# A graph network on one core: the last two gather passes, the first by step instead of by chunk, with a ring of 24 rows, one-hots 12 steps ahead and no spare product

## The chip, the core and the metric

One core of one Trainium2 chip runs the whole program. The metric is the time of one execution on the device in microseconds (us), as the median of several runs. The engines are TensorE (PE; its weight loads are PEld), VectorE (DVE), ScalarE (ACT), GpSimd (POOL) and SyncE (SP). SP and POOL also issue DMAs, POOL the indexed ones.

## The reference

A graph of 6250 nodes and 106,250 edges (50,000 drawn pairs in both directions and one loop for each node, sorted by the target `dst`) goes through four layers, each followed by a residual sum and a layer norm: a graph isomorphism layer, an attention over edges, a layer of degree and edge terms, and the layer that the change is about, which is, shortened:

```python
def _srgnn_conv(x, W, b, src, dst, num_nodes):
    xl = x @ W.T + b
    agg = segment_sum(xl[src], dst, num_segments=num_nodes)
    cnt = segment_sum(ones, dst, num_segments=num_nodes)
    return agg / maximum(cnt, 1.0)[:, None]
input_in  = _srgnn_conv(hidden, W_in,  b_in,  src, dst, n)
input_out = _srgnn_conv(hidden, W_out, b_out, dst, src, n)
# then the gates of a recurrent unit from inputs = [input_in, input_out] and hidden
```

All data is fp32 and 256 wide.

## The kernel before

Eleven stages run one after the other, each ended by a barrier. Four of them gather a row of 256 (or 512) numbers for every edge with indexed DMAs of POOL: `first_gather`, `edge_scores`, and `last_gathers` twice. `last_gathers` makes both sums of the layer above: the inward pass (rows of `src` summed by `dst`) and the outward pass (rows of `dst` summed by `src`).

**Chunks, blocks and steps.** The sorted edges lie in NC = 832 chunks of 128. The nodes lie in NW = 49 blocks of 128. A step adds one chunk's share of one block; a chunk that reaches into the next block takes a second step. There are STEPS = 880 steps in a pass (55 groups of U = 16).

**One step of a pass.** POOL gathers 128 rows (128 KB) into one place of `ring` (line 2083). DVE compares a row of 0 to 127 with the edges' node numbers and so makes four one-hot matrices at once (`hot`, which calls `compare`, line 195). PE multiplies the one-hot with the gathered rows and adds to the block's bank in PSUM (line 2126, tile `l_sums`). An fp32 product is two records of the trace. After each product PE makes a spare product of one column (`push`, line 178) whose result nobody reads. ACT copies a finished block's sum out of PSUM and clears the bank (`take_banks`, lines 186 and 188).

**The inward pass goes by chunk.** POOL gathers 832 chunks, each once, though some serve two steps. Which place of the ring a step reads, and when it may, follow from the block's number in a register (`slot_of`, `chunk_ready`, line 154). SP is the relay: for each chunk it waits for the row, tells PE through `s_here` (line 137), and, eight chunks later, waits for the last step that used the chunk and tells POOL through `s_used` (line 148).

**The outward pass goes by step.** POOL gathers 880 times, PE waits for the row's own semaphore, and POOL waits for `s_sum`, PE's count of steps. In this pass PE, DVE and SP also make the gates for one block in each group of 16 steps (`gate_parts`: four transposes L2027, four products of 512 columns L2039, four of 256 columns L2042; DVE L1999, L2005, L1982, L1994, L2011; a 512 KB write by SP).

**What limits how far the engines run ahead.** The ring has 16 places and POOL asks at every fourth gather, so it is at most 16 and at least 13 gathers ahead of what is used up. `onehot` has HALF = 8 places and DVE makes four of them 4 steps before PE's use:

```python
if u % QUAD == 0 and t + QUAD < 2 * STEPS:
    hot(t + QUAD)
```

Of the kernel before, what the change touches and what calls it, by code (L numbers as in the profile page):

```python
# [12 lines left out]
P = 128  # L13
# [148 lines left out]
def bank_of(block, width):  # L162

    return bass.ds((block % BANKS) * BANK, width)
# [7 lines left out]
    pe.sem_inc(s_sum, 1)  # L172


def push(pe, k, spare):

    ones = k.ones.bitcast(BF16)
    pe.matmul(spare, ones[:, 0:1], ones[:, 0:1], start=True, stop=True)  # L178


def take_banks(act, k, ends, sums, width, place, s_sum, s_taken, s_free, turn=0):

    for w in range(NW):
# [14 lines left out]
def step_tables(nc, k, dst_rows, src_rows, x_rows):  # L198
# [4 lines left out]
    with ExitStack() as ctx:  # L203
# [34 lines left out]
        @block.sync  # L238
        def _(sp):

            sp.dma_start(last_i[:, :], dst_rows[:, P - 1:P].rearrange("c o -> o c"),
                         allow_slow_non_contiguous=True).then_inc(s_last, 16)
            sp.dma_start(k.X, x_rows.rearrange("(w p) d -> p w d", p=P)).then_inc(s_x, 16)

            sp.dma_start(k.src_p, k.src_rows).then_inc(s_x, 16)
            sp.dma_start(k.by_chunk, k.src_cols).then_inc(s_x, 16)
            sp.wait_ge(s_lasts, 4)
            sp.dma_start(k.last_row, k.lasts).then_inc(s_x, 16)
            sp.wait_ge(s_rel, 3 * RT)
# [4 lines left out]
            sp.wait_ge(s_x, 64)  # L254

        @block.gpsimd
        def _(pool):
# [1276 lines left out]
def attr_sums(nc, k):  # L1534

    RING = 4
    with ExitStack() as ctx:
# [6 lines left out]
        s_zeros, s_one, s_src, s_rel, s_hot, s_sum, s_taken, s_free, s_sources = sems(  # L1544
            nc, k, *(f"as_{n}" for n in ("zeros", "one", "src", "rel", "hot", "sum", "taken", "free", "sources")))
# [4 lines left out]
        @block.sync  # L1550
        def _(sp):
            for q in range(BIN_OCTS):
                if q >= RING:
                    sp.wait_ge(s_sum, (q - RING + 1) * OCT + 1)
                    sp.wait_ge(s_src, 2 * (q - RING + 1))
                sp.dma_start(ring[:, q % RING, :, 0:ER], k.bin_rows[q * OCT * P:(q + 1) * OCT * P, :].rearrange(
                    "(p r) d -> p r d", p=P)).then_inc(s_in[q % RING], 16)
            sp.dma_start(k.idx[:, 0:NC], k.src_cols).then_inc(s_sources, 16)
            sp.wait_ge(s_sources, 16)

        @block.scalar
        def _(act):
# [485 lines left out]
    return work  # L2048


def last_gathers(nc, k, a):

    with ExitStack() as ctx:
        room = Arena(k.side)
        ring = room.take([P, U, D])
        flat = ring.rearrange("p u d -> p (u d)")
        onehot = room.take([P, HALF, P])
        lasts_row = room.take([1, NC], I32)
        zeros = room.take([1, BANK])
        sums = psum(nc, ctx, "l3_sums", [P, BANKS * BANK])  # L2060
        spare = psum(nc, ctx, "l3_spare", [1, BANK])
        s_zeros, s_hot, s_sum, s_taken, s_free, s_lasts, s_here, s_used = sems(nc, k, *(f"l3_{n}" for n in (
            "zeros", "hot", "sum", "taken", "free", "lasts", "here", "used")))
        s_row, row0 = k.s_row, k.rows_before
        k.rows_before += NC + 16 * IT
# [5 lines left out]

        @block.gpsimd
        def _(pool):
            for n in range(NC + STEPS):
                u = n % U
                column = k.idx[:, n:n + 1] if n < NC else k.idx2[:, n - NC:n - NC + 1]
                if u % QUAD == 0 and n >= U:

                    if n < NC + U:
                        pool.wait_ge(s_used, n + QUAD - U)  # L2080
                    else:
                        pool.wait_ge(s_sum, STEPS + (n - NC) + QUAD - U + 1)
                pool.indirect_dma_start(ring[:, u, :], None, k.x3_rows, bass.IndirectOffsetOnAxis(  # L2083
                    ap=column, axis=0)).then_inc(s_row[u], 16)

        @block.sync
        def _(sp):
            sp.dma_start(lasts_row, k.last_row).then_inc(s_lasts, 16)
            fold.sync(sp)
            work.load_bias(sp)  # L2090
            sp.sem_inc(s_here, HERE)
            sp.wait_ge(s_lasts, 16)
            lasts = None
            for c in range(NC):
                lasts = relay_chunk(nc, sp, lasts, lasts_row, c, s_row, row0, s_here, s_sum, s_used)
            for c in range(NC - BEHIND, NC):
                lasts = relay_used(nc, sp, lasts, lasts_row, c, s_sum, s_used)
            work.sync(sp)

        @block.scalar  # L2100
# [7 lines left out]
        def _(pe):  # L2108
# [4 lines left out]
            for t in range(2 * STEPS):  # L2113
# [12 lines left out]
                pe.matmul(sums[:, bank_of(node[u] + turn, D)], onehot[:, u % HALF, :], flat[:, bass.ds(at, D)],  # L2126
                          start=False, stop=True, skip_group_check=True).then_inc(s_sum, 1)
# [6 lines left out]
        def _(dve):  # L2134
            def hot(t):

                node = (k.dst if t < STEPS else k.rel2)[:, t % STEPS:t % STEPS + QUAD]
                if t >= HALF:
                    dve.wait_ge(s_sum, t + QUAD - HALF + 1)
                compare(dve, k, onehot[:, t % HALF:t % HALF + QUAD, :], None, node).then_inc(s_hot, QUAD)  # L2140
# [190 lines left out]
def build(nc, k, a):  # L2331
    with ExitStack() as ctx:
# [11 lines left out]
        k.last_row = dram("last_row", [1, NC], I32).ap()  # L2344
# [115 lines left out]
```

## Time and profile before

| what | value |
|---|---|
| median of 3 runs | 6660.27 us (6643.98 to 6661.23) |
| profiled execution, its own time, first to last instruction | 7527.2 us |
| first gather | 60 to 1360 us |
| edge scores | 1942 to 3275 us |
| edge attribute sums (no gathers of POOL) | 4283 to 4591 us |
| inward pass | 4803 to 6037 us |
| outward pass | 6037 to 7327 us |

The profiled execution is one execution with the profiler on; nothing lies around its span but the launch. It took 867 us more than the median of the runs without the profiler. In every list a group of instructions has its busy time, the mean duration of one in ns, and the idle time of its engine just before it, with what ended that idle time. "issue" means that the profile shows nothing that was waited for. The granted clock of TensorE is 1.0 at 2.4 GHz and 0.5 at 1.2 GHz.

### The profile page before, as it was taken

The numbers are of one execution on the slowest core, as the hardware profiler recorded it, in microseconds if no ns is written. First come the engines' busy times: TensorE is split into PE (matmuls) and PEld (weight loads), VectorE is DVE, ScalarE is ACT, GpSimd is POOL, SyncE is SP. The second block draws the span as 40 slices with busy tenths as digits, with TensorE's granted clock in tenths as the row PEclk, the third lists the DMA queues.
The fourth block names the chain that finished last, engine by engine and source line by source line (L and its number), as shares of the span: only waits on it lengthen the run. The fifth ranks groups of instructions, "written<-read, shape, count | busy, mean of one in ns | idle before, by whom it ended". The sixth has DMA issues, their size and how long they took to land. (4 is left out here: it accounts for less than half of the span.)

```text
span 7527.2 us, 81611 instructions
## 1 busy us (share of the span) xinstructions
PE 5373.7 (71%) x17807; PEld 3065.0 (41%) x17807; DVE 3160.7 (42%) x6956; ACT 545.2 (7%) x1542; POOL 4732.4 (63%) x4778
## 2 busy tenths in 40 slices
PE   5666777638765556636566687788888888888887
PEld 2333333525332223324444575433433344444444
DVE  2222444528655556674444567511111123333317
ACT  0000000324000000010000001100000000000004
POOL 5666665664666666677677404766666666666665
PEclk8777777969767777767778899865555588888869
DMA  4444433331688888846667675433333333333445
GB/s 137 133 134 130 124 123 121 128 100 66 214 256 256 265 262 268 266 134 210 210 217 226 205 191 148 126 89 89 90 89 87 89 111 119 119 119 119 123 101 191
DMA packets 693161, 1164.20 MB, mean 155 GB/s; under 512 B 104128, under 2 KB 490285, under 8 KB 692614
## 3 DMA queue, kind: packets, MB, share of 16 engines
q0 software_dynamic: 224288, 633.55, 28.9%
q1 hardware_dynamic: 468344, 525.21, 21.9%
q8 instruction: 217, 3.56, 0.2%
q14 instruction: 202, 1.65, 0.1%
q10 hardware_dynamic: 110, 0.23, 0.0%
HBM read 870.83 MB, written 287.77 MB: 154 GB/s over the span
## 5 line engine op out<-in xcount | busy, mean ns | idle before, releaser
L2126 PE MATMUL l_sums<-big 128*128 (+1 forms) x3520 | 1701.9, 578 | 349.1 <-issue 135.1
L195 DVE TENSOR_TENSOR big<-iota_row,dst_tab 128x512 f32<-128x512 f32 x660 | 458.4, 695 | 2171.3 <-PE l_sums L2126 712.1
L1280 POOL DMA_INDIRECT bin_rows<-staging,place_tab x832 | 979.6, 1177 | 337.4 <-issue 249.1
L1166 POOL DMA_INDIRECT big<-kv_rows,idx_tab x880 | 832.0, 945 | 503.0 <-issue 241.1
L578 POOL DMA_INDIRECT big<-in_x,big x832 | 826.6, 994 | 483.6 <-SPq L148 237.7
L2083 POOL DMA_INDIRECT big<-x_rows,place_tab x880 | 882.3, 1003 | 394.9 <-issue 241.7
L2083 POOL DMA_INDIRECT big<-x_rows,idx_tab x832 | 817.2, 982 | 426.7 <-issue 226.6
L1220 PE MATMUL es_q<-big 128*128 x1760 | 720.9, 536 | 450.3 <-issue 343.3
L2126 PEld LDWEIGHTS l_sums<-big 128*128 128x128 f32 x3520 | 765.2, 259 | 502.0 <-issue 473.7
L612 PE MATMUL l_sums<-big 128*128 x1760 | 723.0, 543 | 331.9 <-issue 235.8
L1504 PE MATMUL ws_sums<-big 128*128 128x264 f32 x1760 | 546.1, 474 | 321.2 <-DVE big L1524 170.9
L1220 PEld LDWEIGHTS es_q<-big 128*128 128x128 f32 x1760 | 380.6, 252 | 747.7 <-issue 714.1
L612 PEld LDWEIGHTS l_sums<-big 128*128 128x128 f32 x1760 | 393.8, 255 | 623.9 <-issue 587.7
L1239 DVE TENSOR_TENSOR big<-es_q,big 128x256 f32<-128x256 f32 x880 | 370.8, 423 | 547.4 <-remote 274.3
L1504 PEld LDWEIGHTS ws_sums<-big 128*128 128x128 f32 x1760 | 400.6, 236 | 467.7 <-issue 384.9
L178 PEld LDWEIGHTS l_spare<-ones 128*1 128x1 bf16 x1760 | 139.7, 79 | 906.7 <-issue 906.7
L1244 DVE TENSOR_REDUCE sims<-big 128x8 f32<-128x256 f32 x880 | 356.1, 410 | 0.0
L1524 DVE TENSOR_TENSOR big<-big,sims 128x1024 f32<-128x1024 f32 x220 | 268.7, 1221 | 180.5 <-DMA big<-v_edge 173.6
L195 DVE TENSOR_TENSOR big<-iota_row,bin_tab 128x512 f32<-128x512 f32 x220 | 151.8, 692 | 440.4 <-PE l_sums L2126 263.8
L178 PE MATMUL l_spare<-ones 128*1 128x1 bf16 x1760 | 289.3, 164 | 3.4 <-issue 3.4
L1581 PE MATMUL as_sums<-sims 128*128 128x129 f32 x1760 | 249.8, 298 | 56.2 <-DVE sims L195 54.9
L1581 PEld LDWEIGHTS as_sums<-sims 128*128 128x128 f32 x1760 | 232.8, 189 | 74.5 <-issue 67.9
(297 smaller groups left out, 5187.4 us busy)
## 6 DMA issues: line engine op xcount, KB each, us to landing
v_edge<-big SPq DMA_DIRECT2D x880, 128.0 KB
big<-v_edge SPq DMA_DIRECT2D x220, 512.0 KB
bin_rows<-big SPq DMA_DIRECT2D x110, 520.0 KB
sims<-bin_rows SPq DMA_DIRECT2D x110, 520.0 KB
staging<-in_edges SPq DMA_DIRECT2D x104, 520.0 KB
gate_rows<-big SPq DMA_DIRECT2D x49, 512.0 KB
big<-gate_rows SPq DMA_DIRECT2D x49, 512.0 KB
big<-kv_rows,idx_tab POOLq DMA_INDIRECT x880
```

The lines of the kernel that those rows point to most:

```text
L178: pe.matmul(spare, ones[:, 0:1], ones[:, 0:1], start=True, stop=True)
L195: return dve.tensor_tensor(out, rows, columns.unsqueeze(2).to_broadcast([P, QUAD, P]), ALU.is_equal)
L578: pool.indirect_dma_start(ring[:, u, 0:D], None, table, bass.IndirectOffsetOnAxis(ap=k.by_chunk[:, c:c + 1], axis=0)).then_inc(s_row[u], 16)
L612: pe.matmul(sums[:, bank_of(node[u], width)], onehot[:, u % HALF, :], flat[:, bass.ds(slot_of(s, node[u], D + 1), width)], start=False, st ...
L1166: pool.indirect_dma_start(ring[:, u, :], None, k.kv_rows, bass.IndirectOffsetOnAxis(ap=k.idx[:, s:s + 1], axis=0)).then_inc(s_row[u], 16)
L1220: pe.matmul(qps[u % 4][:, 0:D], onehot[:, u % HALF, :], query[:, bass.ds(block_at[u] * D, D)], start=True, stop=True).then_inc(s_q, 1)
L1239: dve.tensor_tensor(prod[:, u % 2, :], qps[u % 4][:, 0:D], ring[:, u, 0:D], ALU.mult).then_inc(s_prod, 1)
L1280: pool.indirect_dma_start(k.bin_rows, bass.IndirectOffsetOnAxis(ap=k.place[:, c:c + 1], axis=0), k.staging[:, g % 2, j, :], None).then_inc ...
L1504: pe.matmul(sums[:, bank_of(node[s % U], AW)], onehot[:, s % HALF, :], weighted[:, s % HALF, :], start=False, stop=True, skip_group_check= ...
L1581: pe.matmul(sums[:, bank_of(node[s % U], EW)], onehot[:, s % U, :], ring[:, q % RING, r, 2:2 + EW], start=False, stop=True, skip_group_che ...
L2083: pool.indirect_dma_start(ring[:, u, :], None, k.x3_rows, bass.IndirectOffsetOnAxis(ap=column, axis=0)).then_inc(s_row[u], 16)
L2126: pe.matmul(sums[:, bank_of(node[u] + turn, D)], onehot[:, u % HALF, :], flat[:, bass.ds(at, D)], start=False, stop=True, skip_group_check ...
```

## The change

- The inward pass goes by step, as the outward pass does: POOL gathers 880 rows, not 832, from the table of steps (`idx_tab`, which held the steps' rows for an earlier stage and is no longer overwritten with the chunks'). SP relays nothing, so `relay_chunk`, `relay_used`, the row `last_row` and its loads are gone from this stage. The first gather keeps its relay.
- The ring has 24 places instead of 16 in both passes, each with a semaphore of its own, and POOL asks `s_sum` at every fourth gather.
- There are 16 one-hots instead of 8, and DVE makes them 12 steps ahead instead of 4.
- The spare product is gone from both passes.

```diff
@@ last_gathers @@
-        ring = room.take([P, U, D])
+        ring = room.take([P, LAST_RING, D])          # 24
-        onehot = room.take([P, HALF, P])
-        lasts_row = room.take([1, NC], I32)
+        onehot = room.take([P, LAST_HOTS, P])        # 16
...
         @block.gpsimd
         def _(pool):
-            for n in range(NC + STEPS):
-                u = n % U
-                column = k.idx[:, n:n + 1] if n < NC else k.idx2[:, n - NC:n - NC + 1]
-                if u % QUAD == 0 and n >= U:
-                    if n < NC + U:
-                        pool.wait_ge(s_used, n + QUAD - U)
-                    else:
-                        pool.wait_ge(s_sum, STEPS + (n - NC) + QUAD - U + 1)
-                pool.indirect_dma_start(ring[:, u, :], None, k.x3_rows, ...).then_inc(s_row[u], 16)
+            for t in range(2 * STEPS):
+                place = t % LAST_RING
+                column = k.idx[:, t:t + 1] if t < STEPS else k.idx2[:, t - STEPS:t - STEPS + 1]
+                if place % QUAD == 0 and t >= LAST_RING:
+                    pool.wait_ge(s_sum, t + QUAD - LAST_RING + 1)
+                pool.indirect_dma_start(ring[:, place, :], None, k.x3_rows, ...).then_inc(s_row[place], 16)
...
         def _(sp):
-            sp.dma_start(lasts_row, k.last_row).then_inc(s_lasts, 16)
             fold.sync(sp)
             work.load_bias(sp)
-            sp.sem_inc(s_here, HERE)
-            sp.wait_ge(s_lasts, 16)
-            lasts = None
-            for c in range(NC):
-                lasts = relay_chunk(nc, sp, lasts, lasts_row, c, s_row, row0, s_here, s_sum, s_used)
-            for c in range(NC - BEHIND, NC):
-                lasts = relay_used(nc, sp, lasts, lasts_row, c, s_sum, s_used)
             work.sync(sp)
...
-                if turn:
-                    pe.wait_ge(s_row[u], row0 + NC + 16 * ((t - STEPS) // U + 1))
-                else:
-                    chunk_ready(pe, t, node[u], s_here)
-                at = u * D if turn else slot_of(t, node[u], D)
+                pe.wait_ge(s_row[t % LAST_RING], 16 * (t // LAST_RING + 1))
+                at = t % LAST_RING * D
...
-                push(pe, k, spare[:, 0:1])
...
             def hot(t):
-                if t >= HALF:
-                    dve.wait_ge(s_sum, t + QUAD - HALF + 1)
+                if t >= LAST_HOTS:
+                    dve.wait_ge(s_sum, t + QUAD - LAST_HOTS + 1)
...
-            hot(0)
+            for t in range(0, LAST_LEAD, QUAD):      # LAST_LEAD = 12
+                hot(t)
...
-                if u % QUAD == 0 and t + QUAD < 2 * STEPS:
-                    hot(t + QUAD)
+                if u % QUAD == 0 and t + LAST_LEAD < 2 * STEPS:
+                    hot(t + LAST_LEAD)
@@ attr_sums, the stage that overwrote idx_tab @@
-            sp.dma_start(k.idx[:, 0:NC], k.src_cols).then_inc(s_sources, 16)
-            sp.wait_ge(s_sources, 16)
@@ step_tables @@
-            sp.wait_ge(s_lasts, 4)
-            sp.dma_start(k.last_row, k.lasts).then_inc(s_x, 16)
```

On POOL the two passes stood in this order before (`idx_tab` is the inward pass, `place_tab` the outward one):

```order
L2083 DMA big<-x_rows,idx_tab 128x256 x832
L2083 DMA big<-x_rows,place_tab 128x256 x880
```

and now:

```order
L2072 DMA big<-x_rows,idx_tab 128x256 x880
L2072 DMA big<-x_rows,place_tab 128x256 x880
```

Nothing else moved on POOL; the inward pass has 48 gathers more.

On PE, in the middle of the inward pass before, two steps (the register instructions find the place in the ring, the bank and the waits' values):

```order
L154 REGISTER_ALU x3
L2125 REGISTER_ALU
L2126 ISA x2
L2126 MATMUL l_sums<-big 128x256
L178 MATMUL l_spare<-ones 1x1
L154 REGISTER_ALU x3
L2125 REGISTER_ALU
L2126 ISA x2
L2126 MATMUL l_sums<-big 128x256
L178 MATMUL l_spare<-ones 1x1
```

and now the same two steps:

```order
L2103 REGISTER_ALU
L2104 ISA
L2104 MATMUL l_sums<-big 128x256
L2103 REGISTER_ALU
L2104 ISA
L2104 MATMUL l_sums<-big 128x256
```

The spare product and four register instructions of each step are gone; the order of the products is as it was.

On DVE, the start of the stage before, where L1976 waits for the biases that SP loads:

```order
L2142 MEMSET big 1x512
L195 TENSOR_TENSOR big<-iota_row,dst_tab 128x512
L1976 TENSOR_TENSOR big<-big 128x512
L195 TENSOR_TENSOR big<-iota_row,dst_tab 128x512 x8
L1916 TENSOR_SCALAR xs<-ones,xs 128x128 x4
```

and now:

```order
L2120 MEMSET big 1x512
L189 TENSOR_TENSOR big<-iota_row,dst_tab 128x512 x3
L1966 TENSOR_TENSOR big<-big 128x512
L189 TENSOR_TENSOR big<-iota_row,dst_tab 128x512 x8
L1906 TENSOR_SCALAR xs<-ones,xs 128x128 x4
```

Two more groups of one-hots stand ahead of the first wait, and so every later group stands 8 steps further ahead of its use.

## Rows read from the trace of the kernel before

**Rows 1.** The head of the page.

```profile
span 7527.2 us, 81611 instructions
```

**Rows 2.** Busy PE, PEld, DVE, ACT, POOL by stretch; granted clock, DMA share, GB/s.

```profile
4283.00:4591.00 308.00, 250.65 (x1762) 232.81 (x1760) 188.05 (x542) 26.26 (x98) 0.00 (x0) 0.99 0.72 188
4803.00:6037.00 1234.00, 1047.77 (x2667) 490.21 (x2667) 161.14 (x242) 35.88 (x96) 817.06 (x832) 0.56 0.32 92
6037.00:7190.00 1153.00, 972.88 (x3371) 523.29 (x3370) 359.25 (x587) 33.64 (x90) 797.05 (x794) 0.86 0.40 118
7190.00:7327.00 137.00, 111.72 (x282) 51.88 (x280) 17.23 (x26) 3.57 (x10) 85.38 (x87) 0.55 0.50 88
```

**Rows 3.** The page, costliest groups: POOL's four gather passes.

```profile
L1166 POOL DMA_INDIRECT big<-kv_rows,idx_tab x880 | 832.0, 945 | 503.0 <-issue 241.1
L578 POOL DMA_INDIRECT big<-in_x,big x832 | 826.6, 994 | 483.6 <-SPq L148 237.7
L2083 POOL DMA_INDIRECT big<-x_rows,place_tab x880 | 882.3, 1003 | 394.9 <-issue 241.7
L2083 POOL DMA_INDIRECT big<-x_rows,idx_tab x832 | 817.2, 982 | 426.7 <-issue 226.6
```

**Rows 4.** Who waited for whom, over both passes (us, times, longest).

```profile
DVE big L195 <- PE l_sums L2126: 975.9, 248, 12.4
POOL big L2083 <- SPq L148: 192.5, 95, 6.3
```

**Rows 5.** Timeline of the inward pass, at the granted clock 0.5.

```profile
5316.14 1.22 PE L2126 MATMUL l_sums<-big 128*128 x2
5317.29 0.08 PEld L178 LDWEIGHTS l_spare<-ones 128*1 128x1 bf16 x1 [0.65 <-issue]
5317.39 1.22 PE L2126 MATMUL l_sums<-big 128*128 x2
```

**Rows 6.** Timeline of PE in the first gather, four steps each (x8).

```profile
1000.68 3.72 PE L612 MATMUL l_sums<-big 128*128 x8
1005.34 2.09 PE L612 MATMUL l_sums<-big 128*128 x8
```

**Rows 7.** Timeline of the outward pass: start, duration, [idle before <- what ended it].

```profile
6397.04 0.59 PE L2126 MATMUL l_sums<-big 128*128 128x256 f32 x2
6398.81 0.70 PE L2042 MATMUL gp_g<-sims,big 128*128 128x256 f32 x2
6398.99 0.94 POOL L2083 DMA_INDIRECT big<-x_rows,place_tab  x1 [0.30 <-issue]
6399.97 0.70 PE L2042 MATMUL gp_g<-sims,big 128*128 128x256 f32 x2
6401.12 0.70 PE L2126 MATMUL l_sums<-big 128*128 128x256 f32 x2
6402.49 0.69 DVE L195 TENSOR_TENSOR big<-iota_row,bin_tab 128x512 f32<-128x512 f32 x1 [0.77 <-PE l_sums L2126]
6402.66 1.34 POOL L2083 DMA_INDIRECT big<-x_rows,place_tab  x1 [2.73 <-PE l_sums L2126]
6403.67 0.86 PE L2126 MATMUL l_sums<-big 128*128 128x256 f32 x2 [1.75 <-DVE big L195]
...
6412.02 1.13 PE L2039 MATMUL gp_g<-sims,big 128*128 128x512 f32 x2
6413.60 1.12 PE L2039 MATMUL gp_g<-sims,big 128*128 128x512 f32 x2
6423.69 0.70 PE L2126 MATMUL l_sums<-big 128*128 128x256 f32 x2
6424.41 0.70 PE L2126 MATMUL l_sums<-big 128*128 128x256 f32 x2
```

**Rows 8.** Timeline of the end of the outward pass.

```profile
7313.40 0.94 POOL L2083 DMA_INDIRECT big<-x_rows,place_tab  x1 [0.30 <-issue]
7325.14 1.22 PE L2126 MATMUL l_sums<-big 128*128 128x256 f32 x2 [0.37 <-DMA big<-x_rows,place_tab]
```

More of the change, by code:

```diff
@@ L172, in clear_banks @@
     pe.sem_inc(s_sum, 1)
-def push(pe, k, spare):
-    ones = k.ones.bitcast(BF16)
-    pe.matmul(spare, ones[:, 0:1], ones[:, 0:1], start=True, stop=True)
 def take_banks(act, k, ends, sums, width, place, s_sum, s_taken, s_free, turn=0):
@@ L253, in _ @@
             sp.wait_ge(s_rows, 48)
-            sp.wait_ge(s_x, 64)
+            sp.wait_ge(s_x, 48)
         @block.gpsimd
@@ L1543, in attr_sums @@
         sums = psum(nc, ctx, "as_sums", [P, BANKS * BANK])
-        s_zeros, s_one, s_src, s_rel, s_hot, s_sum, s_taken, s_free, s_sources = sems(
-            nc, k, *(f"as_{n}" for n in ("zeros", "one", "src", "rel", "hot", "sum", "taken", "free", "sources")))
+        s_zeros, s_one, s_src, s_rel, s_hot, s_sum, s_taken, s_free = sems(
+            nc, k, *(f"as_{n}" for n in ("zeros", "one", "src", "rel", "hot", "sum", "taken", "free")))
         s_in = sems(nc, k, *(f"as_in{n}" for n in range(RING)))
@@ L2048, in gate_parts @@
     return work
+LAST_RING = 24
+LAST_HOTS = 16
+LAST_LEAD = 12
 def last_gathers(nc, k, a):
@@ L2054, in last_gathers @@
         room = Arena(k.side)
-        ring = room.take([P, U, D])
+        ring = room.take([P, LAST_RING, D])
         flat = ring.rearrange("p u d -> p (u d)")
-        onehot = room.take([P, HALF, P])
-        lasts_row = room.take([1, NC], I32)
+        onehot = room.take([P, LAST_HOTS, P])
         zeros = room.take([1, BANK])
         sums = psum(nc, ctx, "l3_sums", [P, BANKS * BANK])
[L2061 to L2065, printed above, removed]
+        s_zeros, s_hot, s_sum, s_taken, s_free = sems(nc, k, *(f"l3_{n}" for n in (
+            "zeros", "hot", "sum", "taken", "free")))
+        s_row = sems(nc, k, *(f"l3_row{n}" for n in range(LAST_RING)))
         k.gate = gate_weights(k)
@@ L2073, in _ @@
         def _(pool):
-            for n in range(NC + STEPS):
-                u = n % U
-                column = k.idx[:, n:n + 1] if n < NC else k.idx2[:, n - NC:n - NC + 1]
-                if u % QUAD == 0 and n >= U:
-                    if n < NC + U:
-                        pool.wait_ge(s_used, n + QUAD - U)
-                    else:
-                        pool.wait_ge(s_sum, STEPS + (n - NC) + QUAD - U + 1)
-                pool.indirect_dma_start(ring[:, u, :], None, k.x3_rows, bass.IndirectOffsetOnAxis(
-                    ap=column, axis=0)).then_inc(s_row[u], 16)
+            for t in range(2 * STEPS):
[3 more added lines that the diff above has]
+                    pool.wait_ge(s_sum, t + QUAD - LAST_RING + 1)
+                pool.indirect_dma_start(ring[:, place, :], None, k.x3_rows, bass.IndirectOffsetOnAxis(
+                    ap=column, axis=0)).then_inc(s_row[place], 16)
         @block.sync
         def _(sp):
-            sp.dma_start(lasts_row, k.last_row).then_inc(s_lasts, 16)
             fold.sync(sp)
             work.load_bias(sp)
-            sp.sem_inc(s_here, HERE)
-            sp.wait_ge(s_lasts, 16)
-            lasts = None
-            for c in range(NC):
-                lasts = relay_chunk(nc, sp, lasts, lasts_row, c, s_row, row0, s_here, s_sum, s_used)
-            for c in range(NC - BEHIND, NC):
-                lasts = relay_used(nc, sp, lasts, lasts_row, c, s_sum, s_used)
             work.sync(sp)
@@ L2125, in _ @@
                 pe.wait_ge(s_free, (node[u] & NODE_BITS) + turn * NW)
-                pe.matmul(sums[:, bank_of(node[u] + turn, D)], onehot[:, u % HALF, :], flat[:, bass.ds(at, D)],
+                pe.matmul(sums[:, bank_of(node[u] + turn, D)], onehot[:, t % LAST_HOTS, :], flat[:, bass.ds(at, D)],
                           start=False, stop=True, skip_group_check=True).then_inc(s_sum, 1)
-                push(pe, k, spare[:, 0:1])
                 fold_beside(t)
@@ L2137, in hot @@
                 node = (k.dst if t < STEPS else k.rel2)[:, t % STEPS:t % STEPS + QUAD]
-                if t >= HALF:
-                    dve.wait_ge(s_sum, t + QUAD - HALF + 1)
-                compare(dve, k, onehot[:, t % HALF:t % HALF + QUAD, :], None, node).then_inc(s_hot, QUAD)
+                if t >= LAST_HOTS:
+                    dve.wait_ge(s_sum, t + QUAD - LAST_HOTS + 1)
+                at = t % LAST_HOTS
+                compare(dve, k, onehot[:, at:at + QUAD, :], None, node).then_inc(s_hot, QUAD)
             dve.memset(zeros[:, :], 0.0).then_inc(s_zeros, 1)
-            hot(0)
+            for t in range(0, LAST_LEAD, QUAD):
+                hot(t)
             fold_beside = fold.vector(dve)
@@ L2343, in build @@
         k.bin_rows = dram("bin_rows", [STEPS * P, ER]).ap()
-        k.last_row = dram("last_row", [1, NC], I32).ap()
         k.edge_rows, k.src_rows, k.src_cols = a["edges"], a["src_p"], a["src_c"]
```

## The prediction

> **What bounds the kernel now.** I read the stretches first. In the inward pass POOL is busy 817 of 1234 us and PE 1048, at a mean granted clock of 0.56; in the outward pass it is 797 and 973 of 1153, at 0.86 [rows 2]. Neither is full, so the question is what each waits for.
>
> *POOL's own pace.* A gather that nothing disturbs takes 0.945 us and the next starts 0.30 us later [rows 3, 7], so POOL can't go faster than one gather in 1.246 us. The inward pass adds 817.2 - 832 x 0.946 = 30 us of longer gathers and 426.7 - 832 x 0.30 = 177 us of idle time; the outward pass adds 50 and 131 [rows 3].
>
> *PE's own pace.* At the clock 0.5 a step repeats every 1.25 us (5316.14, 5317.39): the product, then 0.65 us in which the spare's weight load waits, then the spare [rows 5]. At full clock it repeats every 0.72 us [rows 7]. The first gather makes the same product with 257 columns and no spare product: four steps in 3.72 us, 0.93 each, and in 2.09, 0.52 each [rows 6]. So the spare product costs PE 0.32 us a step at the lower clock and 0.20 at the higher, though it computes for only a moment: it stands between a product and the next weight load, which otherwise runs early.
>
> *Whose signals come late.* The gather at 6402.66 stood idle for 2.73 us, and what it waited for is the product that began at 6397.04, so was over at 6397.63: the signal took five us. The compare at 6402.49 and PE's own next product (1.75 us idle at 6403.67) hang on late signals too [rows 7]. Compares waited 976 us for products in these passes, up to 12.4 us at a time [rows 4]. In the stage without gathers PE makes its 880 steps in 308 us at a clock of 0.99 [rows 2], with nothing of the kind. POOL's idle time above 0.30 us a gather is, over its four gather passes, 239 + 234 + 131 + 177 = 781 us [rows 3]. And the profiled execution is 867 us longer than the median of the runs [rows 1]. I read these together: most of the late signals belong to the execution with the profiler on, and the timed runs don't have them. I can't see what delays a signal; POOL's gathers are what the stages with late ones share. It is an inference from two near sums, and the first rival below is that it is wrong. So I make the sum twice.
>
> **The change, on the recorded execution.** If the deeper ring and the longer lead let POOL run without any idle time above 0.30 us, the passes take 880 x 1.246 = 1096 us each, plus longer gathers of 32 and 50: 1128 and 1146. Then some 4 us follow until the last product is done, an estimate from the wait of one gather and one product; now it is 13 (its product starts 11.7 us after the last gather's start and takes 1.2), and it waited for its row, so that signal was late too [rows 8]. Before, the two passes took 1234 and 1290 [rows 2]. In all 1234 + 1290 - 1128 - 1146 - 4 = 246 us less, 7527 - 246 = 7281. But a longer ring doesn't remove late signals, it rides over them. If POOL still needs the outward pass's present 1.45 us a gather ((882 + 395) / 880, [rows 3]), the inward pass takes 880 x 1.45 = 1276, and it is near 7560. I expect the record between, near 7450, and don't rest the prediction on it.
>
> **The change, in the timed runs.** I take the recorded durations and leave the late signals out.
>
> *Inward pass, before.* POOL needs 832 x 1.246 + 30 = 1067 us. PE needs 880 x 1.25 = 1100 at the lower clock, which it has for most of the pass (mean 0.56). So it takes between 1067 and 1100; I take 1085, as some stretches at full clock let PE catch up. *After.* PE needs 880 x 0.93 = 818 at most, POOL 1096 + 32 = 1128. The 48 gathers more cost 60 us on the engine that now sets the pace. Change **+43** (from +28 to +61). The relay's removal saves SP's work and four register instructions a step on PE, none of it on the path once POOL is it: 0.
>
> *Outward pass, before.* A group of 16 steps costs PE at full clock 4 x 1.58 (6412.02 to 13.60, a step with 512 columns of gates) + 4 x 1.16 (6398.81 to 99.97) + 8 x 0.72 [rows 7] and about 1 for the transposes, 17.7 us; at half clock about 1.7 times that, 30. At the mean clock 0.86 (0.72 of the time full) this is 1 / (0.72/17.7 + 0.28/30) = 20.0 us; the busy time says 973/49 = 19.9 [rows 2]. POOL needs 16 x 1.246 + 0.9 = 20.8. These are near each other, and one-hots only 4 steps ahead add small waits: I take 1165 for the pass (1147 if POOL alone decides, 1277 if all waits are real). *After.* Without the spare product PE's group is 17.7 - 3.2 = 14.5 at full clock, near 16.6 in the same mix, well under POOL's 20.8. The pass is POOL's 1147. Change **-18** (from 0 to -130).
>
> *Tail.* The last product's wait was for a late signal [rows 8]; without it PE is as near behind POOL before as after. **0** (to -8).
>
> *Longer gathers.* The gather at 6402.66 took 1.34 us where others take 0.94; a compare had started 0.17 us before it and ended at 6403.18 [rows 7]. The trace shows that a gather that starts inside a compare is held. The 30 and 50 us above are this. The next phase of compares against gathers I can't read off: with none held it is -32 and -50, with each of the 220 compares of a pass holding one by 0.5 us it is +80 and +60. I take **0**: the present rate. The Trainium skill (SBUF — State Buffer, "Who interferes with whom") says a VectorE instruction with two SBUF inputs contends with a GpSimd instruction that reads SBUF and that the loser is blocked; the rows agree, and this would not change the sum.
>
> *The rest.* The load of `idx_tab` that is dropped from the attribute sums was SP's last work there, beside PE's products (that stage has PE busy for 251 of 308 us): 0; uncovered it would be 2 us. The two earlier groups of one-hots cost DVE 1.4 us behind the clearing of the banks: 0. Eight more semaphores to clear at the barrier: 0.
>
> Sum: +43 - 18 + 0 + 0 = **+25**, so 6660 + 25 = **6685 us**, with its own range from 6640 to 6750.
>
> **Rivals.**
> - *The late signals are in every run* (not slower). For it: they are real time in the record, and nothing in the trace says what causes them. Against it: the runs are 867 us shorter, which must come from somewhere, and 781 us lies there. Then the recorded sum holds, -246 at best: about 6420. It makes the change faster once more than 45 of the 308 us of excess idle time in these two passes (177 + 131) are in the timed runs too. Chance 0.13.
> - *PE was further behind than I think in the outward pass.* If PE's group took 21.8 us, the pass was 1200 and the change gains 50 there; with the inward +28 the sum is -30: 6630. For it: PE busy 84% in the record. Chance 0.08.
> - *A gather costs less when it isn't recorded*, say 1.15 us. Then PE set both passes before (1100 and 19.9 x 49 + 120 = 1095) and POOL sets them after (1044 and 1062): about -90, 6570. Against it: the other two gather passes would be shorter by another 160 us, and 781 already fills most of the 867. Chance 0.05.
> - *Every compare holds a gather*: +140, 6800. Chance 0.04.
> - *The clock falls without the spare product.* Then PE takes 14.5 x 1.75 = 25 us a group in the outward pass against 20.8, 49 x 4.6 = +225: 6910. For it: the clock is 0.5 where PE has only the plain steps. Against it: there the spare product was made too, and the clock was still 0.56, and in the last stretch 0.55 with PE busy 112 of 137 us [rows 2]; the spare adds one column to some thousand. It decides if the outward pass's mean clock falls under 0.65. The rule of the Trainium skill that speaks for it (TensorE: Matmul & The Clock Gate, "Why this matters for your kernels": keep TensorE continuously busy, leave no long idle gaps) would have the engine's new idle time bring the clock down. Chance 0.04.
> - The forecast: 0.66.
>
> **The numbers.** Within 0.3% (20 us) is what a measurement of this kernel can't tell from no change. The forecast's own spread puts 0.40 of its 0.66 above +20, 0.24 within, 0.02 below. With the rivals: slower 0.40 + 0.08 = 0.48; same 0.24 + 0.02 = 0.26; faster 0.13 + 0.06 + 0.05 + 0.02 = 0.26. The range from 6510 to 6770 leaves out the late signals in every run (0.13), the clock (0.04) and most of the case of held gathers.
>
> **What would show it.** In the profile after: undisturbed gathers of 0.945 us with 0.30 between them in both passes (steps right), 1760 of them; PE steps every 0.93 us or less when they stand close, no L178; POOL's wait for `s_sum` rarer than before. Wrong would be: mean clock of the outward pass under 0.65; mean gather above 1.03 us; or a time near 6420, which says that the waits that I took for the profiler's are the kernel's.

## The result, and the profile after

The changed kernel takes **6700.5 us** (median of 5 runs, 6682.7 to 6707.4) against 6660.3: a ratio of **1.0064** with a 95% interval of 1.0047 to 1.0082, so 31 to 55 us more. The forecast was 6685. Its profiled execution took 6704.6 us, as long as its timed runs, which the one of before (7527.2) did not. So a second record was taken of the unchanged kernel; it took 6654.7 us, and from here "before" means that record, unless rows of the first are named. A record is called quiet when its span is near 6650 or 6700 us and not near 7500.

Changed kernel: the page's head, then two lines of who waited for whom (us, times, longest), which answer to [rows 1, 4]:

```profile
span 6704.6 us, 72065 instructions
DVE big L189 <- PE l_sums L2104: 1392.3, 374, 6.9
POOL big L2072 <- PE l_sums L2104: 34.7, 114, 0.3
```

POOL's 114 waits for PE are none of them longer than 0.3 us, the idle time that stands before every gather anyway. In [rows 4] it waited for SP's relay up to 6.3 us at a time.

Changed kernel: POOL's four gather passes by group (busy, mean ns | idle, what ended it), against [rows 3]:

```profile
L1158 POOL DMA_INDIRECT big<-kv_rows,idx_tab x880 | 832.1, 946 | 283.1 <-issue 224.0 <-SPq L1168 28.0 <-DVE big L1231 15.8
L570 POOL DMA_INDIRECT big<-in_x,big x832 | 831.1, 999 | 269.7 <-issue 244.0 <-POOLq L108 16.5 <-SPq L148 9.1
L2072 POOL DMA_INDIRECT big<-x_rows,place_tab x880 | 857.4, 974 | 268.1 <-issue 245.9 <-PE l_sums L2104 22.2
L2072 POOL DMA_INDIRECT big<-x_rows,idx_tab x880 | 837.1, 951 | 285.6 <-issue 255.3 <-POOLq L108 17.8 <-PE l_sums L2104 12.5
```

All four passes, also the two whose code is unchanged, now have 0.30 to 0.33 us idle a gather, counting the one wait of 10 to 18 us at the start of a stage; in [rows 3] the unchanged ones had 503.0 and 483.6 us. The unchanged kernel's second record says the same:

```profile
L2083 POOL DMA_INDIRECT big<-x_rows,place_tab x880 | 871.2, 990 | 268.2 <-issue 243.5 <-PE l_sums L2126 24.7
L2083 POOL DMA_INDIRECT big<-x_rows,idx_tab x832 | 797.8, 959 | 262.8 <-issue 249.6 <-POOLq L108 9.6 <-SPq L148 3.7
```

So POOL set the pace of both passes before and after, and a pass is as long as its gathers. The relay's 3.7 us are 12 waits of 0.3 us, so it held nothing up. The view of one line's instructions gives min/median/max ns and the first and the last start. Before, inward and outward:

```profile
L2083 POOL DMA_INDIRECT big<-x_rows,idx_tab x832: 942/947/1463, 4245.5 to 5295.5; - x167
L2083 POOL DMA_INDIRECT big<-x_rows,place_tab x880: 942/947/1461, 5296.8 to 6434.9; - x176
```

and in the changed kernel:

```profile
L2072 POOL DMA_INDIRECT big<-x_rows,idx_tab x880: 942/946/2582, 4261.1 to 5365.0; - x176
L2072 POOL DMA_INDIRECT big<-x_rows,place_tab x880: 942/946/1460, 5366.3 to 6490.5; - x176
```

From the first start to the next pass's first: inward 1051.3, now 1105.2, **+53.9**. First to last start outward: 1138.1, now 1124.2, **-13.9**. From the last gather's start to ACT's copy of the last sum: 17.1, now 14.3, **-2.8**:

```profile
6452.02 0.37 ACT L186 COPY xs<-l_sums 128x256 f32<-128x256 f32 x1 [62.64 <-PE l_sums L2126]
```
```profile
6504.84 0.37 ACT L180 COPY xs<-l_sums 128x256 f32<-128x256 f32 x1 [60.88 <-PE l_sums L2104]
```

The sum is +37, inside the measured 31 to 55. Of the 49.9 us between the two records 15.6 lie ahead of these passes (4261.1 against 4245.5). No cost of the change shows in that: the quiet records of all kernels reach this point between 4240.4 and 4261.1 us, and the changed kernel's own second record (experiment 10) at 4249.8.

A sum of two terms gives all four passes. One is the number of gathers times 1.249 us, the spacing of gathers that nothing holds (0.945 and 0.304). The other is what the longer gathers have above 0.946 us, added up in the trace: 11.3 and 39.3 us before, 5.4 and 25.5 in the changed kernel. That makes 1050, 1138, 1105 and 1125 us, against 1051, 1138, 1105 and 1124 measured. One gather in the changed kernel took 2.58 us. It stands first in the inward pass, beside the three compares in a row that the longer lead puts there (experiment 4 has it too), and makes 1.6 of the 5.4 us.

Last, the same two stretches before and after (busy PE, PEld, DVE, ACT, POOL; granted clock; DMA share; GB/s), against [rows 2]:

```profile
4245.00:5296.00 1051.00, 972.44 (x2687) 460.30 (x2687) 162.63 (x244) 35.88 (x96) 797.31 (x832) 0.64 0.38 108
5296.00:6452.00 1156.00, 1037.44 (x3629) 551.24 (x3629) 379.97 (x611) 36.62 (x98) 871.67 (x881) 0.87 0.45 128
```
```profile
4261.00:5366.00 1105.00, 938.09 (x1811) 416.69 (x1812) 163.05 (x246) 35.87 (x96) 837.10 (x880) 0.62 0.37 108
5366.00:6505.00 1139.00, 920.89 (x2746) 562.40 (x2745) 378.40 (x609) 36.77 (x99) 857.40 (x880) 0.81 0.45 130
```

PE has 117 us less to do outward, and the clock is 0.81 instead of 0.87. Neither shows in the time beyond POOL's 14 us. At the lower clock PE's closest steps are now 0.85 us apart, where before the most frequent distance was 1.24. So the spare product did cost PE time, but time that PE had.

### The profile page after: what moved, and what is told of

It reads as the page before. It is cut to its first block and busy times, and to the rows that moved or that the text cites. A ratio compares the mean times of both kernels' runs of the same rounds, so it can differ in the third digit from the quotient of the medians.

```text
span 6704.6 us, 72065 instructions
## 1 busy us (share of the span) xinstructions
PE 5133.2 (77%) x16047; PEld 2981.3 (44%) x16047; DVE 3169.9 (47%) x6956; ACT 545.6 (8%) x1542; POOL 4753.1 (71%) x4826
## 5 line engine op out<-in xcount | busy, mean ns | idle before, releaser
L2104 PE MATMUL l_sums<-big 128*128 128x256 f32 x3520 | 1594.1, 563 | 384.7 <-DMA big<-x_rows,place_tab 157.0
L1272 POOL DMA_INDIRECT bin_rows<-staging,place_tab x832 | 995.9, 1197 | 284.3 <-issue 249.2
L2072 POOL DMA_INDIRECT big<-x_rows,place_tab x880 | 857.4, 974 | 268.1 <-issue 245.9
L2072 POOL DMA_INDIRECT big<-x_rows,idx_tab x880 | 837.1, 951 | 285.6 <-issue 255.3
L1212 PE MATMUL es_q<-big 128*128 x1760 | 760.9, 564 | 191.4 <-DVE big L1231 188.0
L1496 PEld LDWEIGHTS ws_sums<-big 128*128 128x128 f32 x1760 | 410.3, 241 | 426.7 <-issue 338.7
L1673 POOL DMA_INDIRECT big<-in_L_gnn_z_in,sims x49 | 47.2, 962 | 346.8 <-DVE sims L1765 331.1
L180 ACT COPY big<-l_sums 128x257 f32<-128x257 f32 (+1 forms) x98 | 36.6, 373 | 2124.6 <-PE l_sums L2104 1076.3
```

Of the source, the lines that this page charges most:

```text
L1212: pe.matmul(qps[u % 4][:, 0:D], onehot[:, u % HALF, :], query[:, bass.ds(block_at[u] * D, D)], start=True, stop=True).then_inc(s_q, 1)
L1272: pool.indirect_dma_start(k.bin_rows, bass.IndirectOffsetOnAxis(ap=k.place[:, c:c + 1], axis=0), k.staging[:, g % 2, j, :], None).then_inc ...
L1496: pe.matmul(sums[:, bank_of(node[s % U], AW)], onehot[:, s % HALF, :], weighted[:, s % HALF, :], start=False, stop=True, skip_group_check= ...
L2072: pool.indirect_dma_start(ring[:, place, :], None, k.x3_rows, bass.IndirectOffsetOnAxis(ap=column, axis=0)).then_inc(s_row[place], 16)
L2104: pe.matmul(sums[:, bank_of(node[u] + turn, D)], onehot[:, t % LAST_HOTS, :], flat[:, bass.ds(at, D)], start=False, stop=True, skip_group_ ...
```

## The experiments

Every kernel ran beside the kernel before on one chip, 5 to 12 runs each. Ratios are to that kernel, with 95% intervals. In two of the four groups the kernel before took 6659.2 and 6653.4 us, in the other two 7518.2 and 7520.7 in all of its runs (7486 to 7572). They are kept apart, and "quiet chip" below means one of the first two groups, "late chip" one of the other two.

**1. The kernel before, unchanged (before_again).**

> The kernel before, unchanged, for a record that may be free of late signals, as the one of the changed kernel is. My theory (the late signals belong to one execution with the profiler on): time 6660 within 0.3%, and if this record is quiet too its span is near 6660, with POOL idle 0.30 to 0.34 us a gather in all four gather passes. Inward pass 1067 to 1100 us (PE at half clock with the spare product sets it: PE's step 1.25 us, POOL waits for PE or for SP's relay often), outward pass 1147 to 1180. First rival (POOL set the inward pass before as well): 832 x 1.255 = 1044 to 1050 us inward, and the outward pass longer by as much, 1170 to 1190. Second rival (late signals are in every execution of the kernel before): the record is near 7500 again.

Ratio 0.9996 (0.9987 to 1.0005). The record is the quiet one read above. Inward 1051 and not 1067 to 1100: the first rival holds there, though the outward pass was 1138 and not longer. The theory's 1067 to 1100 falls.

**2. Going by step alone (by_step_only).** The changed kernel with `LAST_RING = 16`, `LAST_HOTS = 8`, `LAST_LEAD = 4` and the spare product:

```diff
+                push(pe, k, spare[:, 0:1])
```

> The first part alone: inward pass by step, 880 gathers, no relay; ring of 16, one-hots 4 steps ahead and spare product as before. My theory: 48 more gathers, of which 17 us hidden before by PE's slower step (PE 1100, POOL 1067); but PE still needs 1.25 us a step at half clock and POOL 1.255, so they are level: +28 to +50 us, 6690 to 6710. First rival (POOL set the inward pass before): +60 us, 6720. Second rival (the relay was a cost of its own, so that without it the pass wins more than 48 gathers cost): at or below 6660.

6715.6 us, **1.0084** (1.0070 to 1.0098), +56 (47 to 65). The passes:

```profile
L2079 POOL DMA_INDIRECT big<-x_rows,idx_tab x880: 942/946/1462, 4260.0 to 5364.3; - x176
L2079 POOL DMA_INDIRECT big<-x_rows,place_tab x880: 942/946/1461, 5365.5 to 6503.8; - x176
```

1105.5 and 1138.3: +54 and 0. The first rival holds: 48 gathers cost their full 60 us (48 x 1.249), less the 6 us by which held gathers cost less (0.952 a gather against 0.959). PE is busy 1050 of the 1105 us at a clock of 0.57, so it is nearly the bound, but POOL never waited for it more than 0.3 us.

**3. The spare product alone (before_no_spare).**

```diff
-                push(pe, k, spare[:, 0:1])
```

> The last part alone on the kernel before: no spare product in the two passes. My theory: PE's step falls from 1.25 to 0.93 us at half clock, so the inward pass becomes POOL's 832 x 1.246 + 30 = 1067 (18 less) and the outward pass loses 10 to 18: 6625 to 6645. First rival (POOL set both passes anyway): 0, 6660. Second rival (the clock falls without the spare): outward pass longer, 6700 to 6850, with a mean granted clock under 0.65 there.

6648.7 us, 0.9987 (0.9978 to 0.9996), -9 (-15 to -3).

```profile
L2082 POOL DMA_INDIRECT big<-x_rows,place_tab x880 | 858.2, 975 | 268.2 <-issue 243.5 <-PE l_sums L2125 24.4 <-SPq L148 0.3
L2082 POOL DMA_INDIRECT big<-x_rows,idx_tab x832 | 804.8, 967 | 263.8 <-issue 251.4 <-POOLq L108 10.6 <-SPq L148 1.8
```

The idle time is as before. What moved is the length of a gather: 0.990 to 0.975 us outward (-13.0) and 0.959 to 0.967 inward (+7.0). So in these passes the spare product's work on PE cost no time; its removal moves when the compares begin against the gathers. The trace counts it: outward, the gathers lengthened by a compare have 11.0 us above 0.946 us instead of 24.9, inward 17.3 instead of 10.3, and those lengthened by the gates' instruction hardly change (14.2 against 13.6). Neither the theory nor a rival said that. The clock rival falls: 0.83 outward, and inward the mean clock is higher without the spare product (0.71 against 0.64), with PE busy 814 us instead of 972.

**4. The spare product and the longer lead (before_lead_no_spare).** As 3, with 16 one-hots and

```diff
-                if u % QUAD == 0 and t + QUAD < 2 * STEPS:
-                    hot(t + QUAD)
+                if u % QUAD == 0 and t + 12 < 2 * STEPS:
+                    hot(t + 12)
```

> The last two parts on the kernel before, by chunk and with the relay and the ring of 16: one-hots 12 steps ahead in 16 places and no spare product. If my sum is right in its parts (+43 for going by step, -18 for the rest of the outward pass, and 18 of PE's slack inward), this keeps the gains and not the price: 6620 to 6640, faster than both kernels. First rival (POOL alone set both passes, the ring and the lead give nothing): 6655 to 6665. Second rival (the longer lead itself costs, as more compares run while a gather's descriptors are written): 6670 to 6700.

6651.2 us, 0.9988 (0.9979 to 0.9997). The passes are those of 3:

```profile
L2082 POOL DMA_INDIRECT big<-x_rows,idx_tab x832: 942/946/2582, 4261.1 to 5318.3; - x167
L2082 POOL DMA_INDIRECT big<-x_rows,place_tab x880: 942/946/1474, 5319.6 to 6444.8; - x176
```

The lead gives 0. The outward pass is 1125.2 us, with the ring of 24 in the changed kernel 1124.2: the ring gives 0 (or 1 us) as well, as far as two kernels that differ in the inward pass too can tell. The last stretch takes 15.1 to 17.2 us in the quiet records with the ring of 16 (experiment 9 apart), and 14.3 and 14.5 in the two of the changed kernel, so 1 to 3 us are left for the ring.

**5 to 7. One part of the change undone at a time (after_spare, after_ring16, after_lead4).**

```diff
-LAST_RING = 24      # after_ring16
+LAST_RING = 16
-LAST_HOTS = 16      # after_lead4, both lines
+LAST_HOTS = 8
-LAST_LEAD = 12
+LAST_LEAD = 4
```

> The changed kernel with the spare product back in both passes; ring 24 and one-hots 12 ahead stay. Changed kernel 6700. My theory (POOL sets both passes and PE has room): PE's step is 1.25 us at half clock against POOL's 1.255, so the inward pass stays or grows by up to 10 us, and the outward pass grows by 0 to 20: 6700 to 6725. Rival (the clock gate: the spare keeps the clock up): mean granted clock higher than 0.62 inward and 0.81 outward and the time under 6690.

> The changed kernel with the ring cut back to 16 places. My theory: POOL waits for PE rarely with either (35 us in all in the changed kernel's record), a row needs about 3 us of 16 x 1.255 = 20 us of ring, so inward 0, and outward up to +20 where PE's groups of gates (17 us in a burst) let it fall behind: 6700 to 6720. Rival (the ring does nothing): 6700 within 0.15%. Rival (a longer ring costs, as more rows are in flight and gathers land later): under 6690.

> The changed kernel with one-hots 4 steps ahead in 8 places again. My theory: PE waits for compares a little in the outward pass, where DVE also serves the gates, and makes it up since it has room: 0 to +15, 6700 to 6715. Rival (the lead moves the compares against the gathers: with 12 steps ahead they start at another phase and hold more or fewer gathers): the mean gather moves off 0.951 inward and 0.974 outward by 0.01 us or more, 9 us of time a pass for each 0.01.

These three met a late chip (the kernel before takes 7518.2 us). Ratios: 1.0027 (1.0011 to 1.0043), 1.0000 (0.9981 to 1.0018), 1.0024 (1.0006 to 1.0041). So they say nothing of parts of 10 us at 6700, but overturned my reading of the first record: its 7527 us were no effect of the profiler. That is the kernel's time there. Whether it is the chip or something about it at that time, the runs don't tell.

One thing beside POOL's idle time sets these records apart: how long a register instruction of PE's own sequencer takes. Over the changed kernel's two passes, first on a late chip (the third record, experiment 12), then on a quiet one (min/median/max ns):

```profile
L2104 PEldq FUSED_REGOPS  x1760: 2/88/1401, 4797.2 to 7309.2; - x196
L2104 PEldq FUSED_REGOPS  x1760: 79/84/110, 4269.4 to 6503.4; - x196
```

In the whole program 105 to 277 of these instructions take over 0.3 us in each of the six late records, and none over 0.13 us in the eight quiet ones. Around 5002 to 5008 us of the first, each takes 0.70 us and PE's steps start 2.80 us apart. So PE itself runs late there, and not only the news of its products. Whether that is the cause or one more effect is open.

**8. Compares with one SBUF input (before_psum_rows).** As 3, and the row of 0 to 127 lies in the freed PSUM bank:

```diff
+            dve.tensor_copy(count_ps[:, 0:P], k.iota_row[:, :]).then_inc(s_count, 1)
+            dve.wait_ge(s_count, 1)
...
-                compare(dve, k, onehot[:, t % HALF:t % HALF + QUAD, :], None, node).then_inc(s_hot, QUAD)
+                compare(dve, k, onehot[:, t % HALF:t % HALF + QUAD, :],
+                        count_ps[:, 0:P].unsqueeze(1).to_broadcast([P, QUAD, P]), node).then_inc(s_hot, QUAD)
```

> The kernel before without the spare product, and the row of 0 to 127 that the compares of the two passes read copied once into the PSUM bank that this frees, so that a compare has one SBUF input instead of two. Theory (a gather that begins inside a compare with two SBUF inputs is held, and that is all that separates the passes of the kernels apart from their number of gathers): the longer gathers vanish (19 us inward, 27 outward in the record without the spare product alone), passes of 832 x 1.2488 = 1039 and 880 x 1.2488 = 1099 us, 6648 - 46 = 6602. Where a chip shows late signals the gathers still fall to 0.945 us, the time by less. Rival (any compare at work holds a gather, whatever its inputs): no difference from the kernel without the spare product, 6648. The Trainium skill (SBUF, section Who interferes with whom) says that a VectorE instruction with at most one SBUF input doesn't contend with GpSimd, which is the theory.

6616.0 us, **0.9934** (0.9920 to 0.9947), 33 us less than the 6648.7 of kernel 3, which was timed in another group beside nearly the same time of before. First what a held gather is: one of experiment 3 beside a compare, and one of the changed kernel beside the gates' instruction (DVE's row, then POOL's):

```profile
5296.98 0.69 DVE L195 TENSOR_TENSOR big<-iota_row,dst_tab 128x512 f32<-128x512 f32 x1 [3.76 <-PE l_sums L2125]
5297.28 1.21 POOL L2082 DMA_INDIRECT big<-x_rows,idx_tab  x1 [0.31 <-issue]
...
5815.39 0.75 DVE L1972 SCALAR_TENSOR_TENSOR big<-sims,big 128x512 f32<-128x512 f32 x1
5815.61 1.36 POOL L2072 DMA_INDIRECT big<-x_rows,place_tab  x1 [0.30 <-issue]
```

Each of the two gathers began inside a DVE instruction with two SBUF inputs and ended 0.82 us after that instruction's end (5297.67 and 5298.49; 5816.14 and 5816.97). Now a compare of this experiment, whose row comes from `l_count` in PSUM, with a gather that begins as far inside it as in the first pair, 0.30 us:

```profile
5019.65 0.69 DVE L195 TENSOR_TENSOR big<-l_count,dst_tab 128x512 f32<-128x512 f32 x1 [3.24 <-PE l_sums L2126]
5019.95 0.95 POOL L2083 DMA_INDIRECT big<-x_rows,idx_tab  x1 [0.30 <-issue]
```

That gather takes 0.95 us. The distance matters: a gather that begins together with a compare isn't held even with two SBUF inputs. In experiment 3 one began 0.02 us after its compare, at 4590.91, and took 0.95 us. Over the passes:

```profile
L2083 POOL DMA_INDIRECT big<-x_rows,idx_tab x832: 942/946/958, 4251.1 to 5289.9; - x167
L2083 POOL DMA_INDIRECT big<-x_rows,place_tab x880: 942/946/1472, 5291.1 to 6403.1; - x176
```

Inward the longest of 832 gathers took 0.958 us, and the pass 1040.0 us (forecast 1039). To count the same thing in both kernels, take the gathers of both passes that began at least 0.10 us after a compare's start and at least 0.20 us before its end. In experiment 3 there are 124, and all of them took over 1.0 us; here there are 117, and none did. Outward the pass is 1112.0 us and not 1099: the gates' `SCALAR_TENSOR_TENSOR` (L1982) still has two SBUF inputs, and 50 of the 57 long gathers began inside it. The other 7 began inside a `TENSOR_SCALAR` of the gates (L1994), which reads one matrix and one number a partition from SBUF. So two full inputs are not the only way to hold a gather, and what about this instruction does it was not tested.

This settles the cause of the lengthening. Did moving the row merely shift the compares? A second count answers that. Two other instructions of the gates have the compare's size and duration (L2005 and L2011, 128x512, 0.69 us) and one input in PSUM in every kernel. By the same measure of distance, 0 of 206 gathers inside them took over 1.0 us in the eight quiet records, against 926 of 926 inside the `TENSOR_TENSOR` and `SCALAR_TENSOR_TENSOR` instructions with two SBUF inputs. All 1056 gathers over 1.0 us in these records had begun inside such an instruction or inside that `TENSOR_SCALAR`. By the Trainium skill (SBUF — State Buffer, "Who interferes with whom") a VectorE instruction with at most one SBUF input, outside the modes in which it uses two ports, does not contend with GpSimd; the trace agrees for the instructions with an input in PSUM. Whether L1994 ran in such a mode, no run here shows.

**9. Spread padding (psum_rows_spread_pad).** As 8, and

```diff
-        dve.memset(fill[:, :, 0:1].bitcast(I32), PAD_DST).then_inc(s_fill, 2)
+        dve.memset(fill[:, :, 0:1].bitcast(I32), PAD_DST).then_inc(s_fill, 1)
+        dve.tensor_copy(fill[:, :, 1:2].bitcast(I32),
+                        k.iota_col[:, 0:1].unsqueeze(1).to_broadcast([P, OCT, 1])).then_inc(s_fill, 1)
```

> The same, and the empty places of the outward pass's table name rows 0 to 127 (the partition's own number) instead of row 0 for all. Theory for the last stretch: in the records the rows of about the last 25 gathers land later and later (from 3 us after their start to 12 to 15), one every 1.65 us against 1.25, since these steps are empty and read row 0 128 times each; with different rows they land after 3 us and the last product starts some 4 us after the last gather instead of 13 to 15: 10 us less than the kernel above, 6592. Rival (the last rows land late for another reason, such as the writes of the gates still in the queue): the tail stays at 13 to 15 us.

6600.8 us, **0.9918** (0.9905 to 0.9932), the fastest kernel of this study. For POOL's last 11 gathers of the changed kernel and last 12 of this one, the time from start to landing (min/median/max), and ACT's copy of the last sum here:

```profile
DMA to landing us min/median/max: 9.3/10.2/12.6
```
```profile
DMA to landing us min/median/max: 2.7/2.7/2.8
6391.54 0.37 ACT L186 COPY xs<-l_sums 128x256 f32<-128x256 f32 x1 [50.96 <-PE l_sums L2127]
```

The last gather starts at 6387.2, so the last stretch is 4.3 us instead of 15.9 in kernel 8. The rival falls. The kernel gained 15 us where 10 were forecast. Another 5 us come from the outward pass (1106.9 against 1112.0), in which fewer gathers happened to be held (39 over 1.0 us instead of 57); nothing in the edit aims at that. A gather of one row 128 times is issued like any other, but in the changed kernel the last products, each waiting for its row, start 1.4 to 1.8 us apart (8 intervals in the 13.0 us from 6490.55 to 6503.59, 1.63 each). By the growth of the landing time about the last 25 steps are such ones.

**10. The changed kernel again (after_again).** No edit.

> The changed kernel once more, beside the kernel before on the chip that the call gets. Theory: where the kernel before takes 6660 us, POOL sets both passes and this is 1.005 to 1.008 of it. Where the kernel before takes 7520 us (late signals in every execution there), a gather takes 1.42 us by step against 1.48 by chunk, so 880 x 1.42 = 1250 inward against 1233, and -12 outward: 1.000 to 1.002. Rival (the deeper ring rides over late signals): on such a chip under 0.997.

6697.7 us, 1.0059 (1.0045 to 1.0072). Its record repeats the first one's stretches: 1105.5 inward, 1123.6 outward, 14.5 to the last copy.

**11 and 12. Step and no spare product, ring 16 and lead 4 (step_no_spare), beside the changed kernel (after_third).**

> The changed kernel with ring 16 and one-hots 4 steps ahead in 8 places: what is left of the change is going by step and no spare product. Theory (POOL sets both passes; the ring and the lead do nothing on a chip without late signals): equal to the changed kernel within 0.15%, passes of 1104 and 1125 us. Rival (the ring and the lead give what is left of the difference, as the compares come at another phase): 10 to 20 us above the changed kernel. Where the chip shows late signals the theory says nothing of these two; there the difference to the changed kernel is what a deeper ring and a longer lead are worth against late signals.

> The changed kernel once more, as the neighbour of the kernel above on the same chip. On a chip where the kernel before takes 6660 us: 1.005 to 1.008 of it. On one where it takes 7520 us: 1.000 to 1.002 of it by the record's pace of a gather, under 0.997 if the deeper ring rides over late signals.

Again a late chip (the kernel before takes 7520.7 us). step_no_spare 1.0007 (0.9984 to 1.0030), the changed kernel **0.9999** (0.9977 to 1.0022): there the change does nothing that can be measured, and ring and lead are worth nothing against late signals either (within 0.4%). The changed kernel there:

```profile
L2072 POOL DMA_INDIRECT big<-x_rows,place_tab x880 | 879.1, 999 | 382.0 <-issue 245.4 <-remote 99.8 <-PE l_sums L2104 36.7
L2072 POOL DMA_INDIRECT big<-x_rows,idx_tab x880 | 858.3, 975 | 401.5 <-issue 251.3 <-PE l_sums L2104 93.4 <-remote 44.0
```

Against [rows 3], 48 more gathers inward come with 25 us less idle time (401.5 against 426.7), so that pass grows by 13 us only (1247 against 1234), and the outward pass is 16 us shorter (first to last start 1260 against 1276). So there going by step costs a quarter of what it costs on a quiet chip. That SP's relay, which stood between two late signals, is what the pass is rid of fits this, as step_no_spare has it too (396.3 us idle inward with ring 16 and lead 4), but no run takes the relay away alone.

## Why the prediction was right, and where it was not

The direction and size hold: +43 and +39 us measured in the two comparisons, +25 forecast. The core of it was right: 48 more gathers on the engine that sets the pace. That the rest came out near is in part luck, as it leaned on PE being close to a bound in both passes, and PE was in neither. By its own steps:

- **Whose signals come late.** The step "most of the late signals belong to the execution with the profiler on" fell. Two records (6654.7, 6704.6) are as fast as the timed runs, and in two groups every timed run had the 7500 us. The sum of 781 us did find the right 867 us; but what it separates is a late chip from a quiet one, and the first record and the three times ahead of the prediction had not met the same. What makes signals late there stays open, and no experiment here was made for it.
- **Inward before, 1085** ("PE needs 1100", "POOL needs 1067"). It was 1051.3. POOL alone set the pace; its bound was 16 us too high, as I took the held gathers of the late record (30 us, here 11), and PE's 1100 was no bound. It holds only if all steps are at the lower clock; mixed as I mixed the outward pass, my own figures (0.72 and 1.25 us, clock 0.56) give an estimate of 1010, under POOL's 1067, and the quiet record's clock of 0.64 gives 910. With that the +43 of this term became **+53.9**: the 48 gathers were nearly in full on the path.
- **Inward after, 1128.** 1105.2: held gathers cost 5 us, not 32. The pace of 1.246 us was right (1.249).
- **Outward, 1165 to 1147, -18.** 1138.1 to 1124.2, **-13.9**. The number is close by luck, and the reason wrong: the 18 us were "small waits" for one-hots, and POOL's waits for PE in that pass were 0.3 us each. The pass was POOL's before too, and what it gained is held gathers, 0.990 to 0.974 us. Experiment 3 shows that the spare product alone does it. Why its removal moves compares to a better phase outward and a worse one inward was not tried.
- **Longer gathers, 0.** This was the term that held the whole outward change. Its mechanism, "a gather that starts inside a compare is held", is what experiment 8 showed, with the condition that the compare has two SBUF inputs and began before the gather; it measured -6 inward and -14 outward. Only its size could not be read off ahead.
- **Tail, 0 (to -8).** -2.8. But "that signal was late too" was wrong: the rows land late in the quiet records too, by the padding of row 0.
- **The recorded execution, "near 7450".** On a late chip the changed kernel's record (experiment 12) is 7510.8 against 7527.2: -16 us. The gathers kept a pace of 1.42 us inward and 1.43 outward, so the branch "near 7560" had the better rule, while the late signals did not give way to the deeper ring.
- **Rivals.** "The late signals are in every run" was half true: on a late chip they are, and the change still isn't faster, so its sum of -246 falls. PE further behind: the second record has POOL waiting 24.7 us for PE outward, never over 0.3. Clock: 0.81 outward, above the 0.65 from which it decides. Of a cheaper unrecorded gather nothing was seen: records and timed medians agree within 0.3%.

## What to carry to other kernels

Before you sum terms, ask if the record comes from the same conditions as the times: compare its span with the timed median, and compare stages with unchanged code. Where indexed DMAs set the pace, count them first (each 1.249 us here, with a ring of 16 or 24 and a lead of 4 or 12). Then look at the longest ones. Here every gather over 1.0 us in the quiet records had begun inside a VectorE instruction that read two operands from SBUF, and moving one input of the compares to PSUM gave 33 us back. Let padding name different rows.

## What was unexpected of the hardware

- A gather that begins 0.1 us or more after a VectorE instruction with two SBUF inputs has begun ends 0.82 us after that instruction's end, as if all but its first 0.13 us came only then; this costs up to 0.5 us. One that begins together with it takes its usual 0.95 us. With one input in PSUM: none of 832 over 0.958 us.
- Gathers of one row 128 times land one every 1.63 us, with different rows each within 2.7 to 2.8 us of its start.
- The same program takes 6655 us in two groups of runs and 7520 in two others, each on a chip of its own, 13% apart. The undisturbed gather is the same (0.945 us); the mean idle time between gathers is 0.43 to 0.60 us instead of 0.30 to 0.33 in the four passes that gather, and register instructions of PE take up to 1.40 us instead of 0.13.
